# Second chunk's carried part of a state-space mixer from (C times B) times values instead of a chunk state, and a re-ordered drain

## The chip, the cores and the metric

One core of a Trainium2 chip runs the whole kernel: one launch, one program on five engines (TensorE = PE, VectorE = DVE, ScalarE = ACT, GpSimd = POOL, SyncE = SP) that meet at semaphores. The metric is device microseconds from start to end.

## The reference, cut to what matters

16 sequences of 256 tokens go through an embedding with attention, a state-space mixer (Mamba-2 style) and a mixture of eight experts. The change touches the mixer's scan `_ssd`: a sequence is two chunks of 128 tokens, with 8 heads of 64 channels and a state of 128.

```python
Y_diag = jnp.einsum('bcln,bcsn,bhcls,bcshp->bclhp', Cc, Bc, Lm, Xc)
decay_states = jnp.exp(a_cs[..., -1:] - a_cs)
states = jnp.einsum('bcln,bhcl,bclhp->bchpn', Bc, decay_states, Xc)
states = jnp.concatenate([jnp.zeros_like(states[:, :1]), states], axis=1)
...
prev_states = jnp.einsum('bhzc,bchpn->bzhpn', decay_chunk, states)[:, :-1]
Y_off = jnp.einsum('bcln,bchpn,bhcl->bclhp', Cc, prev_states, jnp.exp(a_cs))
return (Y_diag + Y_off).reshape(b, l, h, p)
```

With two chunks only the second has a carried part: exp(a_cs) * C2 (B1^T (decay * X1)), where 1 and 2 are the chunks. It is then gated, normalised, projected and added to the residual; then a router picks two of eight experts for each token, rows are scattered to slots in HBM, and each expert runs two products over its slots.

## The kernel before, in words

**Two parts.** The first handles one batch (a sequence of 256 tokens) after the other, in a software pipeline; the second (`experts`) runs the eight experts. Between them lies the drain: the last batch's mixer and routing, the scatter of its rows, and the load of the first expert's rows.

**The pipeline.** Each engine's program is a function `half(p, f, b, t, nf)`, called by `run_batches`. In one half, batch `f` is at its front (attention, input projection, convolution), batch `b`, the one before, is in its middle (the scan, the gate, the output projection), and `t`, two before, at its tail (routing, scatter). `q = 1 - p` is the buffer set of batch `b`. The order of work on an engine is the order in which `half` calls the helpers, and nothing but semaphores moves it. Halves with `f` and `b` are the steady loop, 15 of them; a half with `b` but no `f` is the first half of the drain, and one with neither its last.

**One half on PE, in order** (names are the helpers'): `query_side`, `project_z`, `scores`, `state_inputs` (L1593 transposes B of chunk 1, L1595 makes C B^T inside both chunks, L1597 the running sums), `x_to_rows`, `values`, `segment_sums` 0 and 1, `attend` (L1534, waits for `v` from DVE), `to_v2T`, `segment_sums` 2, `route`, `segment_sums` 3, `chunk_state` (L1633, B1^T times decayed values into bank 3), `own_chunk` 0 (L1643, the part inside chunk 1), `to_hT` (L1495 on `hn`), `from_state` (L1650, C2 times the state into bank 2), `own_chunk` 1, `choices_before`, `to_yT` 0 (L1495 on `y`, waits for the gated `y` of chunk 1 from DVE), `project_dt`, `project_channels`, `to_yT` 1, `project_out`.

**One half on DVE:** `query_max` (L1042, right behind `scores`), `mask_scores` (L1147), `scale_v` (L1051), `times_dt`, `decay_scores` (L1164: decays times the masked scores, one of 128x1024 for each chunk), `norm_1`, `router_in` and `router_top` (small), then `first_y` (L1177 and the gate L1171: y of chunk 1), `carried_y` (L1183: exp(a_cs) times what `from_state` made), `split_hT` (L1066), `second_y` (L1190, L1193 and the gate L1171), `slots_of`, `embedded`, `conv` in three groups among the small steps of a softplus, and `residual`.

**ACT** copies between banks and SBUF: `state_inputs` takes the transposed B to `bs` (L824; in the drain `state_copy`, L815), and `state` the state to `st` (L738). **POOL** makes the decayed values (`decayed_x`, L581), multiplies the values with D (`skip_x`, L588), makes segment inputs, takes roots (`gated_root`, L594), and describes and scatters rows (`describe_rows`, L612 to L616; `scatter_rows`, L625, four indirect DMAs for a batch).

`keep_clock` is a run of PE products whose result nobody reads. The last one before the experts stands behind the transposes of the first expert's rows (L1862).

## Time and profile before

| what | value |
|---|---|
| median of 3 runs | 926.17 us (925.28 to 926.82) |
| the profiled execution | 926.9 us, its span 925.2 us |
| busy, PE / PE weight loads | 904.3 us (98%) / 806.5 us (87%) |
| busy, DVE / ACT / POOL | 633.4 (68%) / 528.6 (57%) / 503.8 (54%) us |
| batches in a steady loop | from 41 to about 500 us |
| drain and start of the experts | from about 500 to 549 us |
| experts | from 549 us to the end; PE busy for 371.9 of the 372.0 us from 549 to 921 |

A busy share is a sum of the spans in which the engine shows an instruction. PE instructions overlap in the trace, so what one costs PE is read from the start of one group to the start of the next. An entry such as `[0.47 <-ACT hn L759]` at the end of a row says that the engine stood idle for 0.47 us before it, and what ended that. A matmul of four-byte floats shows as two records, so x16 in a PE row is eight products.

### The profile page before, as it was taken

How to read it: one execution, taken by the hardware profiler on the slowest of the kernel's cores; microseconds unless marked ns; L12 is line 12 of the kernel's file. 1: busy time of each engine (PE TensorE's matmuls, PEld its weight loads, DVE VectorE, ACT ScalarE, POOL GpSimd, SP SyncE). 2: the span in 40 equal slices, each digit the busy share in tenths (PEclk: the TensorE clock that was granted, in tenths of full speed). 3: DMA queues.
4: the chain of work that ended last, by engine and by line, in shares of the span. 5: the costliest groups of instructions: out<-in, count | busy, mean ns of one | idle time of the engine just before them, and what ended most of it. 6: DMA issues, size and time to landing. Idle time of an engine off the chain costs nothing. (4 is left out here: it accounts for less than half of the span.)

```text
span 925.2 us, 17776 instructions
## 1 busy us (share of the span) xinstructions
PE 904.3 (98%) x5832; PEld 806.5 (87%) x5832; DVE 633.4 (68%) x1698; ACT 528.6 (57%) x1097; POOL 503.8 (54%) x498
## 2 busy tenths in 40 slices
PE   8999999999999999999999979999999999999998
PEld 7888798888888888888888779999999999999997
DVE  1587889888988898889889644646464646464633
ACT  1767776677667766776667434444443434343533
POOL 5656877887778777876775522223232323232343
PEclk9999999999999999999999989999999999999999
DMA  7940011001000000000000044343434342523221
GB/s 211 321 154 17 30 47 34 23 34 34 13 23 14 24 13 23 14 25 12 12 14 5 25 138 122 70 109 74 108 70 112 67 115 63 119 58 79 23 58 46
DMA packets 49398, 59.13 MB, mean 64 GB/s; under 512 B 6304, under 2 KB 44683, under 8 KB 49360
## 3 DMA queue, kind: packets, MB, share of 16 engines
q1 hardware_dynamic: 35920, 42.14, 14.1%
q0 software_dynamic: 13440, 16.50, 10.7%
q8 instruction: 21, 0.34, 0.2%
q14 instruction: 17, 0.14, 0.1%
HBM read 33.62 MB, written 30.67 MB: 69 GB/s over the span
## 5 line engine op out<-in xcount | busy, mean ns | idle before, releaser
L690 POOL DMA_INDIRECT out<-ye,tok_slot x56 | 96.0, 1713 | 250.0 <-DMA out<-ye,tok_slot 128.0
L973 ACT ACTIVATE hf<-bank 128x512 f32<-128x512 f32 x128 | 79.3, 620 | 187.1 <-PE bank L1814 187.0
L1423 DVE TENSOR_TENSOR h_lo<-hf,h_hi 128x512 fp32r<-128x512 f32 x128 | 88.8, 694 | 101.5 <-ACT h_hi L975 100.1
L1812 PE MATMUL bank<-w_hi,h_hi 128*128 128x256 f32 x512 | 146.1, 285 | 0.0
L1813 PE MATMUL bank<-w_lo,h_hi 128*128 128x256 f32 x512 | 144.9, 283 | 0.0
L1814 PE MATMUL bank<-w_hi,h_lo 128*128 128x256 f32 x512 | 144.9, 283 | 0.0
L1122 DVE SCALAR_TENSOR_TENSOR xc<-bank,cw,xc 128x253 f32<-128x253 f32 (+2 forms) x288 | 128.2, 469 | 1.9 <-ACT xc L799 0.4
L1812 PE MATMUL bank<-xe_hi,w_hi 128*128 128x512 f32 x256 | 100.0, 391 | 0.0
L1813 PE MATMUL bank<-xe_lo,w_hi 128*128 128x512 f32 x256 | 99.8, 390 | 0.0
L1814 PE MATMUL bank<-xe_hi,w_lo 128*128 128x512 f32 x256 | 99.7, 389 | 0.0
L1813 PEld LDWEIGHTS bank<-w_lo,h_hi 128*128 128x128 f32 x512 | 98.3, 192 | 0.0
L1812 PEld LDWEIGHTS bank<-w_hi,h_hi 128*128 128x128 f32 x512 | 98.2, 192 | 0.0
L1814 PEld LDWEIGHTS bank<-w_hi,h_lo 128*128 128x128 f32 x512 | 98.2, 192 | 0.0
L625 POOL DMA_INDIRECT slots_dram<-rows,slot x64 | 63.7, 995 | 57.4 <-DVE slot L1271 35.7
L975 ACT ACTIVATE h_hi<-bank 128x512 fp32r<-128x512 f32 x128 | 79.4, 620 | 0.0
L1643 PEld LDWEIGHTS bank<-xdt,seg 128*128 128x128 f32 x512 | 61.0, 192 | 17.2 <-issue 16.5
L1440 DVE TENSOR_SCALAR ye<-bank,w_slot 128x256 f32<-128x256 f32 x58 | 27.9, 481 | 60.3 <-PE bank L1814 58.2
L573 POOL TENSOR_TENSOR seg_hi<-tri,a_hi 128x1024 fp32r<-128x1024 f32 x31 | 58.7, 1895 | 6.5 <-DVE a_lo L1107 6.5
L1643 PE MATMUL bank<-xdt,seg 128*128 128x64 f32 x512 | 60.9, 272 | 0.0
L799 ACT ACTIVATE xc<-bank,cb,cw 128x256 f32<-128x256 f32 x96 | 48.2, 563 | 20.6 <-PE bank L1550 18.7
L1662 PE MATMUL bank<-w_out,yT 128*128 128x256 f32 x256 | 58.2, 379 | 1.1 <-ACT yT L738 1.1
L573 POOL TENSOR_TENSOR seg_lo<-tri,a_lo 128x1024 fp32r<-128x1024 f32 x31 | 58.7, 1894 | 0.0
(223 smaller groups left out, 2352.3 us busy)
## 6 DMA issues: line engine op xcount, KB each, us to landing
w_raw<-w SPq DMA_DIRECT2D x16, 1024.0 KB
slots_dram<-zero_row SPq DMA_DIRECT2D x1, 8320.0 KB, 29.9
xe<-slots_dram SPq DMA_DIRECT2D x15, 520.0 KB, 4.5
out<-hb SPq DMA_DIRECT2D x16, 256.0 KB, 2.1
w_raw<-in_wT SPq DMA_DIRECT2D x2, 644.0 KB, 6.2
out<-zero_row SPq DMA_DIRECT2D x1, 1024.0 KB, 32.1
slots_dram<-rows,slot POOLq DMA_INDIRECT x64
out<-ye,tok_slot POOLq DMA_INDIRECT x64
```

What stands on the lines that cost most here:

```text
L573: ins = g.tensor_tensor(part[p][:, c, :, :], bc(tri[:, :].unsqueeze(1), [P, NH, P]), bc(a_part[p][:, c, :].unsqueeze(2).bitcast(F32), [P, ...
L625: g.indirect_dma_start(slots_dram, bass.IndirectOffsetOnAxis(ap=slot[p][:, 2 * c + k:2 * c + k + 1], axis=0), rows[p][:, c, :], None, boun ...
L690: g.indirect_dma_start(out, bass.IndirectOffsetOnAxis(ap=tok_slot[q][:, j:j + 1], axis=0), ye[q][:, j, :], None, compute_op=ALU.add).then_ ...
L973: sc.activation(hf[m % 2][:, :], h_bank[i % H_BANKS][:, :], ACT.Gelu_apprx_tanh)\
L975: sc.activation(h_hi[:, m, :], h_bank[i % H_BANKS][:, :], ACT.Gelu_apprx_tanh)\
L1122: ins = vc.scalar_tensor_tensor(out=xc[p][:, m, back:], in0=bank[p][XBC_BANK[i]][:, h * L:(h + 1) * L - back], scalar=cw[:, m, TAPS - 1 - ...
L1423: vc.tensor_tensor(h_lo[:, m, :], hf[m % 2][:, :], h_hi[:, m, :].bitcast(F32), ALU.subtract)\
L1643: ins = te.matmul(bank[p][YD_BANK[c]][:, h * HD:(h + 1) * HD], seg[p][:, c, h, :], xdt[p][:, c, h * HD:(h + 1) * HD], start=True, stop=True)
L1662: ins = te.matmul(bank[where][0][:, c * DM:(c + 1) * DM], yT[p][:, c, k, :], w_out[:, k, :], start=(k == 0), stop=(k == KI - 1))
L1812: te.matmul(out_, hi, rhi, start=first_, stop=False)
L1813: te.matmul(out_, hi, rlo, start=False, stop=False)
L1814: return te.matmul(out_, lo, rhi, start=False, stop=last_)
```

## The change

1. PE: `state_inputs` no longer transposes B of chunk 1. In its place it makes B1 times C2, a 128x128 product, in the same part of bank 3. ACT copies it as before, now to `across`.
2. PE: `chunk_state` becomes `across_chunks`. It multiplies `across` with the decayed values into bank 3, and that is at once the carried part. `from_state` is gone, and on ACT the copy `state` to `st`.
3. DVE: `carried_y` reads bank 3, and stands ahead of `first_y`, in the steady loop and in the drain.
4. The drain, POOL: `gated_root` of the last batch but one moves from the last steady half to behind `decayed_x`; `skip_x` waits until DVE has finished the decay products of both chunks; the last batch's rows are described by DVE, between `router_top` and `slots_of`, not by POOL.
5. The drain, PE: the last `keep_clock` before the experts has 3 products instead of 6.

```diff
@@ POOL, half: the drain @@
                     if b:
                         decayed_x(b, q)
+                        gated_root(t, p)
+                        pool.wait_ge(m_ready[KD - 1][q], m_ready[KD - 1].now(b, q))
                         skip_x(b, q, 0)
                         skip_x(b, q, 1)
                         pool.wait_ge(y_ready[q], y_ready.now(b, q))
...
                         second_root(b, q)
-                    describe_rows(t, p)
+                        describe_rows(t, p)
                     scatter_rows(t, p)
                     return
...
                 if not nf:
                     segment_inputs(f, p, 0)
-                    gated_root(b, q)
                     free_rows(t, p)
                     return
@@ ACT @@
             def state_inputs(r, p):
                 act.wait_ge(btg_psum[p], btg_psum.now(r, p))
-                sc.activation(bs[p][:, :], bank[p][3][:, 0:NS], ACT.Copy)
+                sc.activation(across[p][:, :], bank[p][3][:, 0:P], ACT.Copy)
...
-            def state(r, p):
-                act.wait_ge(state_psum[p], state_psum.now(r, p))
-                copy(st[p][:, :], bank[p][3][:, :], st_ready[p])
@@ DVE @@
                     dve.wait_ge(yo_psum[p], yo_psum.now(r, p))
-                    carried_y.last = back.mark(vc.tensor_tensor(heads(y[p][:, 1, :]), heads(bank[p][2][:, :]),
+                    carried_y.last = back.mark(vc.tensor_tensor(heads(y[p][:, 1, :]), heads(bank[p][3][:, :]),
...
+                def describe_rows(t, p):
+
+                    dve.wait_ge(tok_next[1 - p], tok_next.now(t, 1 - p))
+                    dve.wait_ge(ohs_ready[p], ohs_ready.now(t, p))
+                    vc.tensor_copy(rows[p][:, :, C_TOK].bitcast(I32), tok_iota[:, :])
+                    vc.tensor_copy(rows[p][:, :, C_E0], topf[p][:, :, 0])
+                    vc.tensor_tensor(rows[p][:, :, C_W0:C_W0 + 2], top[p][:, :, 0:2],
+                                     bc(linv[p][:, :].unsqueeze(2), [P, KD, 2]), ALU.mult).then_inc(row_info[p], 1)
...
                 if b:
+                    carried_y(b, q)
                     first_y(b, q)
-                    carried_y(b, q)
                 if f:
                     split_hT(f, p)
...
+                if not f:
+                    describe_rows(t, p)
                 if t:
                     slots_of(t, p)
@@ PE @@
                     pe.wait_ge(a_ready[p], a_ready.now(r, p))
-                    te.transpose(bank[where][3][:, 0:P], xc[p][:, KI, 0:P], ident[:, :])
+                    te.matmul(bank[where][3][:, 0:P], xc[p][:, KI, 0:P], xc[p][:, KI + 1, P:2 * P], start=True, stop=True)
...
-                def chunk_state(r, p):
+                def across_chunks(r, p):
...
-                    te.matmul(bank[p][3][:, :], bs[p][:, :], xdec[p][:, :], start=True, stop=True)\
-                        .then_inc(state_psum[p], 1)
+                    te.matmul(bank[p][3][:, :], across[p][:, :], xdec[p][:, :], start=True, stop=True)\
+                        .then_inc(yo_psum[p], 1)
...
-                def from_state(r, p):
-                    pe.wait_ge(st_ready[p], st_ready.now(r, p))
-                    pe.wait_ge(decay_ready[p], decay_ready.now(r, p))
-                    te.matmul(bank[p][2][:, :], xc[p][:, KI + 1, P:2 * P], st[p][:, :], start=True, stop=True)\
-                        .then_inc(yo_psum[p], 1)
...
-                    keep_clock(0, 6)
+                    keep_clock(0, 3)
```

The steady loop on PE, from the chunk state to the transposes of y (`hn` is the normalised front input, `seg` the decays times scores, a row with `waits` names the semaphores). Before:

```order
L1633 MATMUL bank<-xdec,bs 128x512 [waits xdec_ready,bs_ready,decay_ready]
L1643 MATMUL bank<-xdt,seg 128x64 [waits xdt_ready,xs_ready,m0_ready]
L1643 MATMUL bank<-xdt,seg 128x64 x7
L1495 MATMUL bank<-ident,hn 128x128 [waits hn_ready]
L1495 MATMUL bank<-ident,hn 128x128 x3
L1649 REGISTER_ALU [waits st_ready]
L1650 MATMUL bank<-st,xc 128x512 [waits decay_ready]
L1643 MATMUL bank<-xdt,seg 128x64 [waits m1_ready]
L1643 MATMUL bank<-xdt,seg 128x64 x7
```

And now:

```order
L1636 MATMUL bank<-xdec,across 128x512 [waits xdec_ready,bs_ready,decay_ready]
L1646 MATMUL bank<-xdt,seg 128x64 [waits xdt_ready,xs_ready,m0_ready]
L1646 MATMUL bank<-xdt,seg 128x64 x7
L1498 MATMUL bank<-ident,hn 128x128 [waits hn_ready]
L1498 MATMUL bank<-ident,hn 128x128 x3
L1646 MATMUL bank<-xdt,seg 128x64 [waits m1_ready]
L1646 MATMUL bank<-xdt,seg 128x64 x7
```

The product with the state is gone from between the transposes of `hn` and the second chunk's own part.

The same part of the steady loop on DVE, behind the router's small steps. Before:

```order
L1249 TENSOR_TENSOR ohs<-oh 128x16 [waits routing_chain]
L1177 TENSOR_TENSOR y<-bank,xs 128x512 [waits skip_ready,yd_psum]
L83 REGISTER_ALU [waits sz_ready]
L1171 TENSOR_TENSOR y<-y,sz 128x512 [waits back_chain]
L1183 TENSOR_TENSOR y<-bank,ea 128x512 [waits yo_psum]
L1066 TENSOR_TENSOR hT_lo<-hn,hT_hi 128x512 [waits hT_ready]
```

And now:

```order
L1241 TENSOR_TENSOR ohs<-oh 128x16 [waits routing_chain]
L1175 TENSOR_TENSOR y<-bank,ea 128x512 [waits yo_psum]
L1169 TENSOR_TENSOR y<-bank,xs 128x512 [waits skip_ready,yd_psum]
L1163 TENSOR_TENSOR y<-y,sz 128x512 [waits back_chain,sz_ready]
L1058 TENSOR_TENSOR hT_lo<-hn,hT_hi 128x512 [waits hT_ready]
```

The carried part stands one place earlier, and the first chunk's sum and gate one place later.

The drain on POOL, at the last batch's decayed values. Before:

```order
L594 TENSOR_TENSOR rms<-msq,neg_half 128x2 [waits msq_ready]
L581 TENSOR_TENSOR xdec<-xdt,edec 128x512 [waits scattered1,xdt_ready,edec_ready]
L588 TENSOR_TENSOR xs<-xs,dskip 128x512 [waits xs_ready] x2
L605 TENSOR_TENSOR hb<-h,bias_b 128x512 [waits h2_ready,hb_stored1,y_ready]
```

And now:

```order
L579 TENSOR_TENSOR xdec<-xdt,edec 128x512 [waits scattered1,xdt_ready,edec_ready]
L592 TENSOR_TENSOR rms<-msq,neg_half 128x2 [waits msq_ready]
L586 TENSOR_TENSOR xs<-xs,dskip 128x512 [waits xs_ready,m1_ready]
L586 TENSOR_TENSOR xs<-xs,dskip 128x512 [waits xs_ready]
L603 TENSOR_TENSOR hb<-h,bias_b 128x512 [waits h2_ready,hb_stored1,y_ready]
```

The root has moved behind the decayed values, and the products with D wait for `m1_ready`, which DVE gives behind its second decay product.

## Rows read from the trace of the kernel before

**Rows 1.** Windows: length, busy us (instructions) of PE, PEld, DVE, ACT, POOL; then PEclk, DMA
```profile
41.00:474.90 433.90, 429.75 (x2729) 374.23 (x2728) 373.22 (x1169) 309.87 (x669) 329.80 (x337) 1.00 0.11 33
532.00:549.00 17.00, 12.27 (x89) 11.69 (x88) 7.06 (x23) 4.87 (x9) 5.79 (x10) 0.80 0.44 142
```

**Rows 2.** Timeline of PE, one turn: start us, us, what [idle before]
```profile
323.17 1.99 PE L1534 MATMUL bank<-v,probs 128*128 128x256 f32 x8
...
330.99 0.66 PE L1495 MATMUL bank<-ident,hn 128*128 128x128 f32 x4 [0.47 <-ACT hn L759]
331.55 1.12 PE L1650 MATMUL bank<-st,xc 128*128 128x512 f32 x2
332.51 1.89 PE L1643 MATMUL bank<-xdt,seg 128*128 128x64 f32 x16
...
334.37 0.63 PE L1495 MATMUL bank<-ident,y 128*128 128x128 f32 x4
...
350.57 0.27 PE L1593 MATMUL bank<-ident,xc 128*128 128x128 f32 x1
350.68 0.61 PE L1595 MATMUL bank<-xc 128*128 128x128 f32 x4
...
351.74 1.89 PE L1516 MATMUL bank<-wv,xT 128*128 128x256 f32 x8
...
354.49 1.99 PE L1534 MATMUL bank<-v,probs 128*128 128x256 f32 x8
```

**Rows 3.** Timeline of DVE, the same turn
```profile
332.06 0.68 DVE L1177 TENSOR_TENSOR y<-bank,xs 128x512 f32<-128x512 f32 x1
332.78 0.69 DVE L1171 TENSOR_TENSOR y<-y,sz 128x512 f32<-128x512 f32 x1
333.39 0.68 DVE L1183 TENSOR_TENSOR y<-bank,ea 128x512 f32<-128x512 f32 x1
333.99 0.68 DVE L1066 TENSOR_TENSOR hT_lo<-hn,hT_hi 128x512 fp32r<-128x512 f32 x1
...
350.78 0.68 DVE L1042 TENSOR_REDUCE nmax<-bank 128x2 f32<-128x512 f32 x1
```

**Rows 4.** Timelines of DVE and PE, the turn behind it
```profile
363.32 0.68 DVE L1177 TENSOR_TENSOR y<-bank,xs 128x512 f32<-128x512 f32 x1
...
364.83 0.64 PE L1495 MATMUL bank<-ident,y 128*128 128x128 f32 x4
...
385.25 1.99 PE L1534 MATMUL bank<-v,probs 128*128 128x256 f32 x8
```

**Rows 5.** Timeline of DVE, end of the first full turn
```profile
71.34 0.69 DVE L1042 TENSOR_REDUCE nmax<-bank 128x2 f32<-128x512 f32 x1 [1.62 <-PE bank L1525]
```

**Rows 6.** L1164 over all turns (ns min/median/max); timelines in the drain, last batch's scan
```profile
L1164 DVE TENSOR_TENSOR seg<-seg,gm x32: 1224/1230/2115, 45.8 to 509.9; 128x1024 f32<-128x1024 f32 x32
...
507.96 4.04 DVE L1164 TENSOR_TENSOR seg<-seg,gm 128x1024 f32<-128x1024 f32 x2
508.90 4.01 POOL L588 TENSOR_TENSOR xs<-xs,dskip 128x512 f32<-128x512 f32 x2
...
513.50 0.69 DVE L1171 TENSOR_TENSOR y<-y,sz 128x512 f32<-128x512 f32 x1
```

**Rows 7.** Timelines of DVE and POOL in the drain, the last scatters
```profile
532.49 0.17 DVE L1271 TENSOR_SCALAR slot<-sl 128x4 int32<-128x4 f32 x1
532.57 0.98 POOL L625 DMA_INDIRECT slots_dram<-rows,slot  x1 [0.30 <-issue]
...
534.98 0.99 POOL L625 DMA_INDIRECT slots_dram<-rows,slot  x1 [0.82 <-issue]
```

**Rows 8.** Timelines of PE and DVE at the start of the experts
```profile
546.12 2.77 PE L1482 MATMUL bank<-ident 128*128 128x128 f32 x12
546.99 0.69 DVE L1451 TENSOR_TENSOR xe_lo<-bank,xe_hi 128x512 fp32r<-128x512 f32 x1
...
548.54 0.59 PE L1812 MATMUL bank<-xe_hi,w_hi 128*128 128x512 f32 x1
```

More of the change, by code:

```diff
@@ L237, in lm_block @@
         gm = pair("gm", [P, KD, P])
-        bs = pair("bs", [P, NS])
+        across = pair("across", [P, P])
         xdec = pair("xdec", [P, DI])
-        st = pair("st", [P, DI])
         h2 = pair("h2", [P, KD, DM])
@@ L327, in lm_block @@
         m_ready = [signal(f"m{c}_ready") for c in range(KD)]; skip_ready = signal("skip_ready", 2)
-        state_psum = signal("state_psum"); st_ready = signal("st_ready")
         yd_psum = signal("yd_psum", 2); yo_psum = signal("yo_psum")
@@ L814, in state_copy @@
                 act.wait_ge(btg_psum[p], btg_psum.now(r, p))
-                sc.activation(bs[p][:, :], bank[1 - p][3][:, 0:NS], ACT.Copy)
+                sc.activation(across[p][:, :], bank[1 - p][3][:, 0:P], ACT.Copy)
                 copy(ea[p][:, :], bank[1 - p][3][:, 3 * P:3 * P + NH], bs_ready[p])
@@ L890, in half @@
                     late_rows(b, q)
-                    state(b, q)
                     square(b, q, 0)
@@ L933, in half @@
                     normed(f, p)
-                if b:
-                    state(b, q)
                 if f:
@@ L1331, in half @@
                 if b:
+                    carried_y(b, q)
                     first_y(b, q)
-                    carried_y(b, q)
                 if f:
@@ L1713, in half @@
                     keep_clock(p, DRAIN["state"])
-                    chunk_state(b, q)
+                    across_chunks(b, q)
                     own_chunk(b, q, 0)
-                    from_state(b, q)
                     own_chunk(b, q, 1)
@@ L1767, in half @@
                     segment_sums(b, q, 3)
-                    chunk_state(b, q)
+                    across_chunks(b, q)
                     own_chunk(b, q, 0)
@@ L1773, in half @@
                     to_hT(f, p)
-                if b:
-                    from_state(b, q)
                 if b:
```

## The prediction

> **What bounds the kernel now.** I read the stretches first. The experts keep PE busy throughout, and the change touches no instruction of theirs; they only begin sooner or later. In the steady loop PE is busy for 429.75 of 433.90 us and DVE for 373.22 [rows 1]. That looks like PE alone, so that a product taken from PE would come off the time. I then read the timelines of PE and DVE beside each other over two turns, to see who is late for whom. The reader is to follow three points of a turn: `attend` (start 323.17, 354.49, 385.25), the start of the y steps on DVE (332.06 and 363.32, call it Y), and the first transposes of y on PE (334.37 and 364.83) [rows 2 to 4].
>
> - From `attend` to Y: 8.89 and 8.83 us.
> - From Y to the transposes of y: 2.31 and 1.51 us. DVE has the gated y of chunk 1 at 332.78 + 0.69 = 333.47, which is Y + 1.41 [rows 3]. So in the second turn PE begins as soon as DVE is done; in the first it comes 0.9 us later than it could.
> - From the transposes of y to `values`: 351.74 - 334.37 = 17.37 us of PE work with no idle entry, and from there to the next `attend` 2.75 us [rows 2].
> - DVE goes from Y to `query_max` in 350.78 - 332.06 = 18.72 us [rows 3], without an idle entry as well.
>
> So two chains go round, PE's and DVE's, within half a microsecond of each other, and `attend` waits for whichever is later. Two turns take 385.25 - 323.17 = 62.08 us, 31.04 each. From Y to `attend` it is 22.43 us in one and 21.93 in the other, mean 22.18. In the second the PE chain would have allowed 1.51 + 17.37 + 2.75 = 21.63; what it took, 21.93, is the DVE chain. I take 21.93 as the floor that DVE sets.
>
> **The product with the state (steady loop).** Removed from PE: from its start to the next group's, 332.51 - 331.55 = 0.96 us [rows 2]. Added: a product for a transpose in `state_inputs`. The transpose holds PE for 350.68 - 350.57 = 0.11 us; two products behind it last 0.61 us together with their tail, so one is at most 0.30 [rows 2]. The addition is 0.11 to 0.19; I take 0.11, since the tail overlaps the next group. Net 0.85 us off PE for each batch. The product itself lies between `to_hT` and the own part of chunk 2, ahead of the transposes of y.
>
> Without it PE reaches the transposes of y at 334.37 - 0.96 = 333.41, Y + 1.35, or sooner, because the idle 0.47 us before `to_hT` [rows 2] is not in every turn. But the change puts `carried_y` ahead of `first_y`. It holds DVE for 333.99 - 333.39 = 0.60 us [rows 3], and the y of chunk 1 is now done at Y + 0.60 + 1.41 = Y + 2.01. With 0.06 us for the semaphore PE begins at Y + 2.07. **PE stands still for 0.7 us or more, and in the second kind of turn it begins 0.56 us later than it does now.** The rest is 17.37 + 0.11 + 2.75, so `attend` comes at Y + 22.30. That is above DVE's floor of 21.93. A turn is 8.86 + 22.30 = 31.16 us against 31.04: 0.12 us longer. Bounds: DVE's floor, 8.86 + 21.93 = 30.79, 0.25 shorter; and everything as in the first kind of turn with the addition on top, 8.89 + 22.43 + 0.19 = 31.51, 0.47 longer. I take the middle value because each of its terms has its row. There are 13 such turns (`attend` of the third batch to that of the sixteenth): **+1.6 us** (-3.3 to +6.1).
>
> The first full turn is different. There `query_max` waited 1.62 us for PE [rows 5], so DVE has room and the 0.85 us comes off: **-0.8 us** (0 to -0.85).
>
> The copy of the state on ACT goes away and gives nothing: ACT waits for PE right behind it, for the transposes of `hn`. `across_chunks` is the old first product with other operands, so it costs the same. The carried part is there long before DVE asks for it: it is made ahead of `own_chunk` 0.
>
> **The drain: skips behind the decay products.** Now DVE's two decay products take 4.04 us for two, while POOL's two skips take 4.01 beside them [rows 6]. Over all turns the same DVE instruction takes 1.23 us in the median, and 2.1 at most [rows 6]: 0.8 us of its 2.0 here is a wait for POOL. With the skips held back, the second decay product ends about 0.8 us sooner. Not all of it arrives: `first_y` needs the first skip, about 1.0 us of POOL behind `m1_ready`. On DVE there lie the residual sum and now `carried_y` in that time, about 1.4 us, so they cover it. The gate of chunk 1, at 513.50 now [rows 6], would come at about 513.1 to 513.3; the second y gains about 1 us, but PE only asks for it behind the first projection. I take **-0.5 us** for the chain up to the last batch's rows, between 0 (the skips then just push `first_y`) and -1.05. The root that moves is 0.7 us of POOL between `decayed_x` and the wait for DVE, and nobody waits for it there.
>
> The decay product and the skips take turns rather than share, 1.0 us each. The Trainium skill says so of the shared port in "SBUF — State Buffer", section "SBUF: two separate sides": a DVE operation with two inputs in SBUF and a GpSimd operation exclude each other for a whole instruction. By that rule the moved skips would now meet the gate of chunk 1, also of two SBUF inputs, and hold it until the second skip ends; that would leave 0.3 us of the gain and make the time 0.2 us later. I stay with -0.5, inside its range.
>
> **The drain: rows described by DVE.** POOL's fourth scatter starts at 532.57 and lasts 0.98; the fifth starts at 534.98 [rows 7]. Otherwise the next starts 0.30 us behind the end of one, at 533.85. Four small POOL instructions and a wait go away: 534.98 - 533.85 = **-1.1 us**. The last batch's slots are ready at 532.66 [rows 7], and half a microsecond sooner with the step before, so they cover. On DVE the three small operations lie where it waits 1.0 us for PE's counts. Range -0.8 to -1.1, if the slots are late next.
>
> **The last keep_clock.** Six products now take 548.54 - 546.12 = 2.42 us at the low clock, 0.40 each; the split of the rows that the first expert product needs ends at 546.99 + 0.69 = 547.68 [rows 8]. With three, PE is done at 547.3 and waits until about 547.74: 0.8 us sooner. But the stretch has a mean granted clock of 0.80 [rows 1]: 17 us x 0.20 / 0.5 = 6.8 us at 1.2 GHz, and the rise to 2.4 GHz lies about where the products begin now. Up to 1 us of expert products would run at half speed and give 0.5 us back. I take **-0.4 us** (-0.8 to +0.8, if the clock rises later after the small pause). The Trainium skill, "TensorE: Matmul & The Clock Gate", section "Why this matters for your kernels", has continuous work on PE as the way to the full clock; by it the three products taken away are work that counts towards the rise. It speaks against this edit, and would make the time up to 0.8 us longer rather than 0.4 shorter.
>
> **Sum.** +1.6 - 0.8 - 0.5 - 1.1 - 0.4 = -1.2 us. The profiled execution of before would go from 926.9 to 925.7. Its time stands 0.7 us above the median of 926.17, so the median to compare with goes to **925.0 us**. A measurement of this kernel tells about 0.2%, 1.9 us, from no change, and this lies within it.
>
> **Rivals.**
>
> *DVE alone sets the turn (B).* The wait for y is absorbed because PE needs less than I read. Then the turn is 30.79 us: 13 x -0.25 = -3.3, with the rest -2.8: -6.1 us, 920.1. For it: half of the turns already run at that floor. Against it: 17.37 us is the same number in both kinds, so it is PE work and not waiting. Chance 0.2.
>
> *PE is the bound, and all of its saving arrives (C).* 0.85 x 14 = -11.9, with -2.0 of the drain: -13.9, 912.3. For it: 98% busy. Against it: DVE has no idle entry between Y and `query_max`. The Trainium skill, "Perfetto Trace Analysis", section "Identifying the Most-Contended Engine", has one look for the engine of the highest occupancy and work on it; by that rule this is the case. Chance 0.04.
>
> *Slower: POOL's skips fall in front of DVE's second decay product in every turn (D).* The place is the decay product of chunk 2 in the steady loop, behind `attend`. In the drain it took 2.0 us with POOL ahead [rows 6]; the price is 0.8 us where the router's small steps do not absorb it. It decides if `attend` to Y grows from 8.86 to over 9.2 us. At half the price, 0.4 x 13 = +5.2 on top of -1.2: +4.0, 930.2. For it: `attend` moves later against `query_max`, and POOL's roots hang on the latter. Against it: both kinds of turn had the same 8.8 to 8.9 us. Chance 0.12.
>
> *The edits of the drain do not add up (E):* only the scatters gain, the rest is hidden behind PE's projections: 13 x 0.12 - 0.8 - 1.1 = -0.3, 925.9. Chance 0.1, no change.
>
> **How the numbers follow.** The forecast has 0.54, with its own range 923 to 927; a third of it lies more than 1.9 us below the median of now. Faster: 0.18 + 0.2 (B) + 0.04 (C) = 0.42. Within 0.2%: 0.36 + 0.1 = 0.46. Slower: 0.12 (D). The range reaches down to B, 920.3, and up to 928.2, where the forecast's turn would be 0.25 us longer than I say; C and most of D stay out.
>
> **What the changed profile would show.** Right: PE idle about 0.7 to 1.4 us before the transposes of y in every turn, ended by DVE's gate; Y to `attend` near 22.3 us in all turns, no more alternation; turns of 31.1 to 31.2 us; in the drain decay products of 2.0 and 1.2 us; 0.3 us between the fourth and fifth scatter; the first expert product about 1.6 to 2.4 us closer to the drain's start. Wrong: turns below 31.0 us, with `attend` waiting for v behind `query_max` (B) or no idle before y's transposes (C); `attend` to Y above 9.2 us (D); a pause of the clock that reaches far into the experts.

## The result and the profile after

The changed kernel takes **938.43 us** in the median of four runs (935.2, 935.6, 941.27, 952.05) against 926.29 for the kernel before (925.28 to 926.82); the ratio is 1.012, with a 95% interval of 1.007 to 1.017. The run of 952.05, at the lowest granted clock of the four (0.969), is left out of the ratio, and the other three have a median of 935.6. So the change makes the kernel slower by 1.2%, where I forecast no change or a small gain, and the time lies above my range (920.3 to 928.2). The profiled execution took 935.6 us with a span of 933.9, against 926.9 and 925.2.

The head of the changed kernel's page:

```profile
span 933.9 us, 17711 instructions
...
PE 899.7 (96%) x5810; PEld 810.8 (87%) x5810; DVE 633.5 (68%) x1701; ACT 520.5 (56%) x1081; POOL 495.7 (53%) x494
```

PE's busy time went down from 904.3 to 899.7 us, and the span went up by 8.7. The windows of the changed kernel show in which stage: length, busy us (instructions) of PE, PEld, DVE, ACT and POOL, then the granted clock (PEclk), DMA share, GB/s.

```profile
74.39:487.34 412.95, 396.54 (x2536) 352.98 (x2536) 351.63 (x1106) 282.47 (x612) 304.44 (x322) 0.98 0.08 23
487.34:514.17 26.83, 25.49 (x165) 22.84 (x165) 22.35 (x72) 17.02 (x38) 14.65 (x17) 0.94 0.01 3
514.17:538.24 24.07, 21.89 (x158) 19.17 (x158) 18.19 (x53) 11.08 (x22) 10.36 (x15) 1.00 0.07 23
538.24:556.93 18.69, 14.49 (x111) 13.47 (x110) 8.38 (x34) 6.45 (x12) 7.89 (x8) 0.91 0.39 126
```

The first window is the 13 turns from the `attend` of the third batch to that of the sixteenth. It is 412.95 us long; before it was 403.56 (75.06 to 478.62). The granted clock there is 0.98, where before it was 1.00 [rows 1]. From the last `attend` to the end it is 446.5 us in both kernels. The whole loss lies in the loop, and the granted clock is lower there.

Nine of the 13 turns (from one `attend` to the next) take 31.11 to 31.44 us, mean 31.25. The other four take 32.88, 32.98, 32.98 and 32.89. First one of the nine, from its `attend` at 138.37 on: timeline of PE.

```profile
146.17 0.66 PE L1498 MATMUL bank<-ident,hn 128*128 128x128 f32 x4 [0.46 <-ACT hn L758]
...
149.39 0.66 PE L1498 MATMUL bank<-ident,y 128*128 128x128 f32 x4 [0.72 <-DVE y L1163]
149.88 0.96 PE L1562 MATMUL bank<-w_dt,hn 128*128 128x8 f32 x8
...
166.91 1.89 PE L1519 MATMUL bank<-wv,xT 128*128 128x256 f32 x8
...
169.66 1.99 PE L1537 MATMUL bank<-v,probs 128*128 128x256 f32 x8
```

And DVE in the same turn:

```profile
147.25 0.68 DVE L1175 TENSOR_TENSOR y<-bank,ea 128x512 f32<-128x512 f32 x1
147.85 0.68 DVE L1169 TENSOR_TENSOR y<-bank,xs 128x512 f32<-128x512 f32 x1
148.64 0.69 DVE L1163 TENSOR_TENSOR y<-y,sz 128x512 f32<-128x512 f32 x1
```

This is the turn that was foretold: the y steps start at `attend` + 8.88, the transposes of y come 2.14 later, then 17.52 and 2.75. The chunk-1 part of y stands behind `carried_y`, and PE waits 0.72 us for it (1.24 to 1.29 in the nine turns where `hn` came without a wait, all four slow ones among them); before, no transposes of y in the loop waited [rows 2, 4].

Now a slow turn, PE's timeline from 114.97 on:

```profile
114.97 0.17 PE L1693 MATMUL bank<-oh_sum,ones_b 128*128 128x8 bf16 x1
116.40 0.66 PE L1498 MATMUL bank<-ident,y 128*128 128x128 f32 x4 [1.27 <-DVE y L1163]
116.90 0.96 PE L1562 MATMUL bank<-w_dt,hn 128*128 128x8 f32 x8
...
118.26 0.28 PE L1553 MATMUL bank<-hT_hi,w_in_lo 128*128 128x256 f32 x1
118.38 0.34 PE L1553 MATMUL bank<-hT_lo,w_in_hi 128*128 128x256 f32 x1
118.52 0.41 PE L1553 MATMUL bank<-hT_hi,w_in_hi 128*128 128x256 f32 x1
118.73 0.42 PE L1553 MATMUL bank<-hT_hi,w_in_lo 128*128 128x256 f32 x1
```

The channel products stand 0.12 us apart up to 118.38 and 0.21 behind it. The windows say why:

```profile
115.00:118.40 3.40, 2.13 (x24) 2.04 (x21) 3.19 (x5) 1.56 (x4) 2.77 (x6) 1.00 0.37 61
118.50:121.80 3.30, 3.30 (x18) 3.30 (x17) 2.48 (x10) 1.44 (x5) 0.66 (x1) 0.50 0.08 17
122.00:125.00 3.00, 3.00 (x26) 2.95 (x25) 2.84 (x14) 1.51 (x3) 2.13 (x3) 1.00 0.25 89
```

From 118.5 to 121.9 the granted clock is at 1.2 GHz, and 2.4 GHz on both sides. The trace has five such stretches of 3.4 us, at 118.5, 214.0, 309.6, 435.9 and 500.8 us, each 2.0 to 2.3 us behind the start of y's transposes; before had none up to 541.96. Four are the slow turns, each about 1.7 us longer; the fifth lies behind the last `attend` and lengthens its window (26.83 us at a clock of 0.94; 25.42 us before).

At another place, between the last scatters and the experts, both kernels have a stretch at 1.2 GHz: 6.8 us from 541.96 before, 3.4 us from 548.6 in the changed kernel.

### The profile page after: what moved, and what is told of

It is laid out like the page before. It is cut to its first block, busy times and chain, and to the rows that moved or that the text cites. A ratio compares the mean times of both kernels' runs of the same rounds, so it can differ in the third digit from the quotient of the medians.

```text
span 933.9 us, 17711 instructions
## 1 busy us (share of the span) xinstructions
PE 899.7 (96%) x5810; PEld 810.8 (87%) x5810; DVE 633.5 (68%) x1701; ACT 520.5 (56%) x1081; POOL 495.7 (53%) x494
## 4 chain that ended last, share of the span: by engine, by line
PE 81%; DVE 9%; issue 4%; ACT 3%; POOL 1%; PEld 1%; another core or an unknown queue 0%; DVEq 0%; POOLq 0%; ACTq 0%
PE bank L1806 13%; PE bank L1807 13%; PE bank L1808 13%; PE bank L1553 12%; PE bank L1659 6%; PE bank L1498 5%; PE bank L1537 3%; PE bank L1528 3%; PE bank L1519 3%; PE bank L1617 3%; PE bank L1512 3%; PE bank L1562 1%; PE bank L1818 1%; PE bank L1680 1%; DVE y L1163 1%
## 5 line engine op out<-in xcount | busy, mean ns | idle before, releaser
L798 ACT ACTIVATE xc<-bank,cb,cw 128x256 f32<-128x256 f32 x96 | 48.7, 561 | 30.4 <-PE bank L1553 21.8
L1553 PE MATMUL bank<-hT_hi,w_in_hi 128*128 128x256 f32 x192 | 61.1, 318 | 0.0
```

What stands on the lines that cost most here:

```text
L1553: ins = te.matmul(dst, *((w_, h_) if transposed else (h_, w_)), start=first_ and n == 0, stop=last_ and n == 2)
```

## Experiments

Theory from here on: the pause before y's transposes lets the clock fall, and nothing else in the change costs. "Drops" are stretches at 1.2 GHz in the loop of the profiled execution, one that falls behind the transposes of y after the last `attend` included. Y is the start of the y steps on DVE. A row of waits has PE's line, the instruction waited for, then us in total, times, and the longest in us.

**E1: the old order of the y steps (in the drain too), the rest as changed.** The product with the state wrote bank 2, the new carried part is in bank 3, where chunk 1's y is transposed; that is what ties `carried_y` to the front. So the transposes go to bank 2, and `to_xT` also waits for `carried_y`.

```diff
-        XS_BANK, YD_BANK, YT_BANK = (2, 1), (1, 0), (3, 1)
+        XS_BANK, YD_BANK, YT_BANK = (2, 1), (1, 0), (2, 1)
...
-                    carried_y(b, q)
                     first_y(b, q)
+                    carried_y(b, q)
...
                         pe.wait_ge(yT_ready[q], yT_ready.now(b, q, 1))
+                        pe.wait_ge(back_chain, Chain(pe, back_chain, BACK_LINKS, b, q).value(2))
```

> The changed kernel with the old order of the y steps (first_y, then carried_y; the transposes of chunk 1's y go to bank 2, since bank 3 still holds the carried part, and to_xT waits for carried_y). Theory 1, the clock: PE's pause of 1.3 us before the transposes of y is what pulls the granted clock down in some turns. Here the pause shrinks to about 0.7 us (the gated y comes at Y + 1.4, PE is there at Y + 0.6), so the drops go away, a turn is DVE's 30.8 us, and the median is 920 to 923 us. Rival, theory 2: any pause of PE near this size drops the clock, or the saving of PE is what makes PE look idle: then low stretches stay in the loop, and the time is above 926 us although the turns without a drop take 30.8 us.

Measured: **920.53 us** (919.72 to 921.09), ratio 0.9945 [0.9929, 0.9962]. No drop. Turns of 30.69 to 31.01 us, the transposes of y 1.47 us behind the y steps' start. Waits of PE from 75 to 478 us, the window, and a turn:

```profile
PE bank L1498 <- ACT hn L758: 5.6, 12, 0.5
PE bank L1498 <- DVE y L1163: 0.8, 2, 0.6
```
```profile
75.00:478.00 403.00, 395.86 (x2548) 348.07 (x2547) 352.96 (x1106) 282.58 (x613) 317.94 (x323) 1.00 0.08 23
```
```profile
205.44 0.66 PE L1498 MATMUL bank<-ident,hn 128*128 128x128 f32 x4 [0.47 <-ACT hn L758]
...
207.99 0.66 PE L1498 MATMUL bank<-ident,y 128*128 128x128 f32 x4
```

The pause has moved ahead of the transposes of `hn`, it is there in 12 of the 13 turns, and the clock stays at 2.4 GHz. This version beats both kernels. Its span is 7.2 us shorter than that of the kernel before: 2.3 in the loop, 0.9 ahead of it and 4.0 behind it, where it has no stretch at 1.2 GHz ahead of the experts.

**E2: the changed kernel with five idle products in the pause.**

```diff
                 if b:
+                    for _ in range(5):
+                        te.matmul(bank[q][2][:, 0:P], ident[:, :], ident[:, :], start=True, stop=True)
                     to_yT(b, q, 0)
```

> The changed kernel with five products that nobody reads (128x128, into bank 2 of the batch) ahead of the transposes of chunk 1's y, in the steady loop: they fill about 1.1 of the 1.3 us in which PE waits for DVE. Nothing that others wait for moves. Theory 1, the clock: no low stretch in the loop, all turns 31.2 us, median 926 us or up to 1.5 below. Rival, theory 2: the time is lost by the later y itself or by other waits, the clock only follows: then the turns stay mixed, 31.2 and 32.9 us, and the median stays at 935 to 941 us.

Measured: **927.04 us** (926.28 to 928.7), ratio 1.0015 [1.0006, 1.0025]. No drop. PE's timeline:

```profile
115.44 1.36 PE L1776 MATMUL bank<-ident 128*128 128x128 f32 x10
116.85 0.66 PE L1498 MATMUL bank<-ident,y 128*128 128x128 f32 x4
```

Turns are 31.11 to 31.23 us, as in the changed kernel's turns without a drop, and the transposes still come at Y + 2.13. Five products that compute nothing and shorten nothing take 9.3 us off the span (933.9 to 924.6): 7.6 in the loop and 2.1 behind it, with 0.4 more ahead of it. The dependencies and the place of y are those of the changed kernel, so this isolates the clock. (One of its ten executions, 928.7 us, ran at a mean clock of 0.994, the others at 0.996 to 1.000.) (A product of four-byte floats is two records; one is 0.22 us here, and five fill 1.1 us. The 0.11 us that I gave for one in E5, E7 and E9 is wrong.)

**E3: the kernel before with only `carried_y` put ahead of `first_y`.**

> The kernel before with carried_y ahead of first_y and nothing else. PE still has the product with the state, so its pause before the transposes of y should be 0.5 us or less in one kind of turn and 0.6 in the other. Theory 1: the clock stays at 2.4 GHz in the loop; a turn grows from 31.04 to 31.2 to 31.5 us (y is 0.6 us later, and in half of the turns PE was waiting for it), median 928 to 932 us. Rival: the order alone makes low stretches as the whole change does: above 934 us.

Measured: **935.55 us** (932.52 to 938.1), ratio 1.0094 [1.0074, 1.0115]. Five drops. I was wrong, the rival right. Waits and a window of PE, and the pause ahead of the first drop (at 149.9):

```profile
PE bank L1495 <- DVE y L1171: 5.0, 13, 0.5
PE bank L1495 <- ACT hn L759: 1.9, 4, 0.5
```
```profile
75.00:478.00 403.00, 396.11 (x2496) 346.50 (x2495) 343.11 (x1081) 279.96 (x608) 296.29 (x314) 0.98 0.08 23
```
```profile
148.19 0.66 PE L1495 MATMUL bank<-ident,y 128*128 128x128 f32 x4 [0.50 <-DVE y L1171]
```

Turns without a drop take 31.0 us, with one 32.8 to 32.9, and the turn behind one 31.8. So two lines in another order, with all products kept, cost about as much as the whole change (9.3 us; its spans are 936.4 against 933.9). And E3 has as much of PE's waiting in the loop (403.00 - 396.11 = 6.9 us) as E1 (7.1 us), which had no drop. The total of the pauses does not decide: the four slow turns of E3 each have one pause, 0.37 to 0.50 us ahead of y, and the turns of E1 have about 0.5 us in all.

**E4: the kernel before with only the edits of the drain** (skips behind the decay products, rows described by DVE; six idle products as before).

> The kernel before with the edits of the drain on POOL and DVE alone: the moved root, the skips behind the decay products, the last rows described by DVE. The last keep_clock keeps its six products. From the changed kernel's trace: 0.5 us at the first scatter and 1.2 us among the scatters, 1.7 us in all, so a median of 924.6 us; the clock in the loop is as before. Rival: the experts' start does not follow the scatters (PE comes late out of its 38 filling products), then 926 us.

Measured: **924.99 us** (924.37 to 925.52), ratio 0.9987 [0.9977, 0.9996]. The scatters come 1.28 to 1.37 us apart throughout. In this execution the stretch at 1.2 GHz ahead of the experts is missing as well, so part of the gain may be the clock's. E1 differs from E4 by the product, its banks and the shorter `keep_clock`, so the product in the right order is worth 4.5 us.

**E5: E3 with three idle products** ahead of the transposes of y (edit as in E2, in another bank), and **E6: the changed kernel with two instead of five.**

> The kernel before, with carried_y ahead of first_y as in the order-alone run, and three idle 128x128 products (0.11 us each, 0.33 in all) into a free bank ahead of the transposes of y in each turn. The order-alone run took 935.55 us, with five stretches at 1.2 GHz behind a pause of 0.4 to 0.5 us at this place. Theory 1 (the clock made nearly all of that loss): no stretch at 1.2 GHz in the loop, turns of 31.0 us as in the turns of the order-alone run without one; 31.0 against 31.04 now for 13 turns is nothing, so 926 to 928 us. Theory 2 (the order costs by DVE alone, and the clock is a bystander): 934 us or more, since the fillers take nothing off DVE. If three products are too few, some of the five stretches stay, 1.7 us each.

> The changed kernel with two idle 128x128 products ahead of the transposes of y where the run with five had none of the stretches at 1.2 GHz: the pauses there go from about 0.66 and 1.27 us to about 0.4 and 1.0 us. Theory 1 (what counts is how long PE is without work at this place): the pauses left are as long as those of the order-alone run (0.4 to 0.5 us), which had five stretches, so 3 to 5 stay and the time is 932 to 938 us. Rival (a few products at this place are enough whatever pause is left): no stretch, 927 us as with five.

Measured, E5: **932.01 us** (929.59 to 932.05), ratio 1.0061 [1.0044, 1.0078]. No drop in the profiled execution (929.59 us). Turns are 31.18 us: three products are 0.66 us, 0.2 more than the pause. That is 13 x 0.14 = 1.8 us over before, and the first full turn is 0.7 longer (30.62 against 29.90): 2.5, which is also the difference of the spans (927.7 against 925.2). The three other executions took 932.0 us, at a mean granted clock of 0.994 against 0.996; what lay between them and the profiled one no trace shows. Theory 1 holds for the drops of the profiled execution, but the median is 4 us above what I gave.

E6: **932.71 us** (930.45 to 936.8), ratio 1.0061 [1.004, 1.0081]. Four drops and one in the drain, at 524.8; the waits of PE for y that are left:

```profile
PE bank L1498 <- DVE y L1163: 7.2, 13, 0.7
```

Its four executions took 936.8, 933.2, 932.22 and 930.45 us at mean granted clocks of 0.987, 0.993, 0.992 and 0.994. The mean clock, and with it, as I read it, the number of drops, differs from execution to execution. That fits the scatter: 5.6 and 6.4 us in E3 and E6, 6.1 in the changed kernel, 1.2 to 3.2 in the others. The changed kernel itself: 935.6 and 935.2 us at 0.989 and 0.987, 941.27 at 0.979.

**E7: E1 with six idle products ahead of the first expert product** in place of three.

> The version with the old order of the y steps (920.53 us), with six idle products again ahead of the first expert product instead of three. With three, PE waited 1.1 us there for DVE's split, at the full clock. Theory 1 (this edit is worth nothing, since three products of 0.11 us fit into the wait): 920.5 us, the wait shorter by 0.33 us, the clock unchanged. Rival (the prediction's step): 0.4 us later, 920.9, or more if the clock is low there and each product takes 0.2 to 0.4 us.

Measured: 921.94 us (920.98 to 923.32), ratio 0.9956 [0.9941, 0.9971]; E1 had 0.9945 with an interval that overlaps. It doesn't separate them. PE in the two kernels, E1 first:

```profile
539.53 0.83 PE L1485 MATMUL bank<-ident 128*128 128x128 f32 x6
541.44 0.49 PE L1807 MATMUL bank<-xe_hi,w_hi 128*128 128x512 f32 x1 [1.08 <-DVE xe_lo L1454]
```
```profile
539.99 1.50 PE L1485 MATMUL bank<-ident 128*128 128x128 f32 x12
542.71 0.49 PE L1807 MATMUL bank<-xe_hi,w_hi 128*128 128x512 f32 x1 [1.21 <-DVE xe_lo L1454]
```

In both PE waits for DVE's split behind its idle products, so they aren't on the path there. From the eighth scatter to the first expert product it takes 8.56 (E1), 8.88 (E4, six) and 8.98 us (E2, three) where the clock is at 2.4 GHz there, and 9.64 to 10.54 (changed kernel, E6, E7, before) where a stretch at 1.2 GHz falls into it; where the stretch reaches past the first expert product it is 8.42 (E10) and 9.18 (E3). E7's falls at 533.9, before the edited products run.

**E8: the changed kernel with the dt products ahead of the transposes of y**, and **E9: the five idle products of E2 behind those transposes.**

```diff
-                if b:
-                    to_yT(b, q, 0)
                 if not b:
                     keep_clock(q, FILL["dt"])
                 if f:
                     project_dt(f, p)
+                if b:
+                    to_yT(b, q, 0)
+                if f:
                     project_channels(f, p, 0)
```

> The changed kernel, with PE's eight small dt products (0.81 us, now behind the transposes of y) put ahead of them, so that PE works through most of its pause. Nothing is added. The chain of PE behind the transposes becomes 0.81 us shorter: Y + 2.13 + 17.52 - 0.81 + 2.75 = Y + 21.59, below the 22.0 us that DVE needs (turns of 30.9 us in the run with the old order of the y steps). The pause goes from 0.7 to 1.3 us to 0 to 0.5. Theory 1 (the pause at this place pulls the clock down, and shortening it below what the old order left is enough): no or one stretch at 1.2 GHz, turns of 30.9 us, 920 to 922 us. Rival (it is the run of small products around this place that does it, whatever stands between them): three to five stretches, 2 us each on top, 926 to 931 us.

> The changed kernel with the same five idle 128x128 products as in the run that had no drop, but behind the transposes of y instead of ahead of them. The pauses of 0.7 to 1.3 us stay whole; only work is added, 5 x 0.11 = 0.55 us per turn on PE's chain, 7 us over 13 turns (turns of 31.75 us). Theory 1 (the length of the pause ahead of y decides): three to five stretches at 1.2 GHz as in the changed kernel, 942 to 946 us. Rival (the work of PE around this place decides, and the pause is only a part of it): no or one stretch, 933 to 936 us.

(The dt products are four, in eight records; they take 0.81 us together as stated.)

E8: **931.18 us** (929.55 to 932.7), ratio 1.005 [1.0033, 1.0067]. Three drops in the loop and one in the drain, at 520.2. The transposes of y no longer wait, and yet the clock falls; the rival was right on the drops, and the time is 0.2 us above its range. PE's waits:

```profile
PE bank L1498 <- ACT hn L758: 3.5, 7, 0.6
PE bank L1562 <- ACT hn L782: 3.4, 13, 0.3
```

What is left is a pause of 0.2 to 0.3 us, now between the router's and the dt products, both of 8 columns.

E9: **953.64 us** (952.59 to 955.7), ratio 1.0305 [1.0287, 1.0323]. No drop:

```profile
149.32 0.66 PE L1498 MATMUL bank<-ident,hn 128*128 128x128 f32 x4 [0.48 <-ACT hn L758]
...
152.54 0.66 PE L1498 MATMUL bank<-ident,y 128*128 128x128 f32 x4 [0.72 <-DVE y L1163]
153.03 1.28 PE L1777 MATMUL bank<-ident 128*128 128x128 f32 x10
```
```profile
75.54:474.00 398.46, 379.68 (x2468) 334.61 (x2468) 327.58 (x1022) 258.73 (x567) 285.22 (x301) 1.00 0.08 23
```

PE waits 0.72 us ahead of y in 12 of the 13 turns (1.24 in the first), longer than in E3, and more in all than in any other kernel (18.8 us of 398.5), at a full clock. So the theory that the length of the pause decides is refuted. The rival that work of 1.1 us beside the pause is enough fits, but is not shown alone: the turns also became 1.8 us longer. And the three other executions ran at mean granted clocks of 0.993 to 0.998, so some of them may have had drops. The time itself is far off both expectations: the turn is 33.1 us, not 31.75, because 1.11 us were added, not 0.55, and `attend` now follows `values` after 3.4 to 3.5 us instead of 2.75: it stands behind segment sums that wait for DVE (`gm`, 4.4 us in 12 waits), which came late with the turn.

**E10: E1 with the dt products ahead of the transposes of y** (edit as in E8).

> The version with the old order of the y steps (920.53 us, no stretch at 1.2 GHz in the loop, although PE pauses 0.5 us ahead of the transposes of hn in every turn), with one thing changed: PE's eight dt products (8 columns each) go ahead of the transposes of y. hT is 0.3 us late for them, as in the run with the dt products first. So a pause of about 0.3 us comes to lie among the smallest products, and nothing is added; DVE sets the turn as before. Theory 1 (a pause pulls the clock down where it lies among the products of 8 columns and the transposes of y, however short, and not at the transposes of hn): three to five stretches at 1.2 GHz, 926 to 931 us. Rival (the pause ahead of the transposes of y was what counted, or the total of the pauses: here about 0.8 us a turn, less than in the changed kernel): no stretch, 920.5 us.

Measured: **923.57 us** (921.96 to 924.83), ratio 0.9973 [0.9962, 0.9984]. One drop in the loop (at 271.8; that turn takes 32.37 us, the others 30.7 to 31.0). PE:

```profile
144.12 0.66 PE L1498 MATMUL bank<-ident,hn 128*128 128x128 f32 x4 [0.47 <-ACT hn L758]
...
146.45 0.17 PE L1693 MATMUL bank<-oh_sum,ones_b 128*128 128x8 bf16 x1
146.89 1.03 PE L1562 MATMUL bank<-w_dt,hn 128*128 128x8 f32 x8 [0.27 <-ACT hn L782]
147.78 0.63 PE L1498 MATMUL bank<-ident,y 128*128 128x128 f32 x4
```

A pause of 0.27 us at this place came with one drop, while 0.47 us ahead of `hn`, in the same turns, had brought none in E1. The median is 3 us above E1's; in the spans (920.6 against 918.0) the loop has 1.2 of the difference, and 1.1 lie behind it, in part because a stretch at 1.2 GHz from 541.5 on reaches into the experts. The time lies between both expectations: the place matters, but a pause this short brings fewer drops than I said.

All kernels side by side. "Pause" is PE's waiting in one turn between the router's products and the first channel product, "work beside it" what was added there; "+ 1" is a further drop in the drain (E6 at 524.8, E8 at 520.2), behind a wait of 0.78 us for the copy of the transposed y.

| kernel | pause, us | work beside it, us | drops | us |
|---|---|---|---|---|
| before / E4 | 0 | 0 | 0 / 0 | 926.3 / 925.0 |
| E1 | 0 (two turns up to 0.6) | 0 | 0 | 920.5 |
| E2 | under 0.1 | 1.1 | 0 | 927.0 |
| E5 | 0 | 0.66 | 0 | 932.0 (profiled 929.6) |
| E10 | 0.27 | 0 | 1 | 923.6 |
| E8 | 0.2 to 0.3 | 0 | 3 + 1 | 931.2 |
| E3 | 0.3 to 0.5 | 0 | 5 | 935.6 |
| E6 | 0.2 to 0.7 | 0.45 | 4 + 1 | 932.7 |
| changed kernel | 0.7 to 1.3 | 0 | 5 | 938.4 (935.6 without the run of 952.05) |
| E9 | 0.7 to 1.2 | 1.1 | 0 | 953.6 |

The table leaves out the stretch at 1.2 GHz around the last scatters and the load of the first expert's rows, 3.4 or 6.8 us long. E1, E2 and E4 have none; all the others have one. It makes the way from the last scatter to the first expert product, or the start of the experts, 0.6 to 2 us longer, so differences of 1 to 2 us between rows can come from it.

## Why the prediction was wrong

**The step that failed** is "PE stands still for 0.7 us or more", in the part on the product with the state. I had the pause, its cause and its length right (0.72 and 1.27 us), and priced it at its own length, 0.56 us in every second turn. Its other price, what the granted clock does behind it, was not in the sum; I thought of the clock only at the last `keep_clock`. It is 6.7 us in the loop, four turns of 1.68, and 1.4 us behind it. E2 confirms it: with the pause filled the same kernel takes 927.0 us. The "what would make it wrong" named a clock pause in the experts, not one in the loop. What I had weighed on the clock stood beside the wrong edit: the Trainium skill, "TensorE: Matmul & The Clock Gate", section "Why this matters for your kernels", has continuous work on PE as the way to the full clock. In the loop, work put into the pause kept the full clock (E2), but unbroken work is not needed for it: E1 had it with 7.1 us of waits in 403, E9 with 18.8 in 398. For the last `keep_clock`, where I named it, no run here shows an effect.

**The turn.** Predicted 31.16 us, from 8.86 + 2.07 + 17.37 + 0.11 + 2.75. The turns without a drop have 8.8 to 8.9, then 2.13 + 17.52 + 2.75; the mean is 31.25. Each term is within 0.07 us. Over 13 turns that is +2.7 instead of +1.6. The rest of the loop's loss is 4 drops of 1.68 us, 6.7; together 9.4, which is 412.95 - 403.56.

**The first full turn:** -0.8 foretold, -0.64 measured (29.26 us against 29.90).

**The skips behind the decay products:** -0.5 foretold, and -0.5 measured, by luck. From DVE's last `gm` to the first scatter it is 24.07 us (514.17 to 538.24), against 24.58 before. The two decay products take 3.25 us against 4.04 [rows 6], with the skips behind:

```profile
518.05 3.25 DVE L1156 TENSOR_TENSOR seg<-seg,gm 128x1024 f32<-128x1024 f32 x2
...
523.39 0.69 DVE L1163 TENSOR_TENSOR y<-y,sz 128x512 f32<-128x512 f32 x1
```
```profile
521.38 2.04 POOL L586 TENSOR_TENSOR xs<-xs,dskip 128x512 f32<-128x512 f32 x2 [0.62 <-DVE seg L1156]
```

But in E4, which has this edit with the old product and the old order, the stretch is 24.58 us: the second decay product takes 1.21 us there too, but nothing is gained, and `first_y` waits 0.44 us for the skip. In the changed kernel `carried_y` covers that wait, as I said, but the gain is not from there: E1 has the old order, the same wait of 0.44 us, and still only 24.00 us.

```profile
499.82 0.42 DVE L1139 TENSOR_TENSOR gm<-bank,tri 128x256 f32<-128x256 f32 x1 [0.93 <-ACT ea L737]
...
523.82 1.07 POOL L623 DMA_INDIRECT slots_dram<-rows,slot  x1 [2.21 <-DVE slot L1263]
```

What E1 has and E4 has not is the new product with its banks, so the 0.5 us belong to it, and the moved skips gave nothing. The new order alone costs here: 25.24 us in E3. The Trainium skill's rule on the shared port ("SBUF — State Buffer", section "SBUF: two separate sides") would, as I forecast it, have had the gate wait for the second skip. The gate starts at 523.39, 0.78 us behind the step ahead of it as in the kernel before, and the second skip ends at 523.42; so no wait shows here. The root that moved takes 1.71 us of POOL, not 0.7, but nobody waits for it, as foretold.

**The rows described by DVE:** -1.1 foretold, -1.2 measured (first to eighth scatter 9.05 us against 10.22), and E4 shows the same (9.07). The fifth scatter now follows after 0.30 us [rows 7]:

```profile
543.46 0.97 POOL L623 DMA_INDIRECT slots_dram<-rows,slot  x1 [0.30 <-issue]
```

**The last keep_clock:** -0.4 foretold; nothing measured. In the kernel before, where the six products ran at 1.2 GHz, PE came to the first expert product without a wait [rows 8]. But with three products and a stretch of 6.8 us as well, E6 and E8 take 10.54 and 10.43 us from the last scatter to that product, against 9.69 before. In the changed kernel PE came late out of its 38 idle products (it started them late itself, `issue`), and then stood for DVE:

```profile
549.70 4.02 PE L1485 MATMUL bank<-ident 128*128 128x128 f32 x25 [0.43 <-issue]
...
554.43 0.83 PE L1485 MATMUL bank<-ident 128*128 128x128 f32 x6
556.93 0.49 PE L1806 MATMUL bank<-xe_hi,w_hi 128*128 128x512 f32 x1 [1.67 <-DVE xe_lo L1454]
```

**The gains of the drain** were there, 1.7 us (0.5 of them from the product), and were given back by the fifth drop (1.4 us) and 0.3 us in the experts: 446.5 us from the last `attend` to the end in both kernels.

**The rivals.** B, DVE alone as the bound with turns of 30.79 us and 920.1 us, is not what the change does, but it is close to what E1 does: 30.86 us in the mean, 21.8 to 22.0 from Y to `attend` where I had read 21.93 as DVE's floor. My reading of the floor was right. That E1's 920.5 us lies so near B's 920.1 is in part luck: the loop gave 2.3 us, not 3.3, and the drain more than I had put there. If DVE is the floor, further savings on PE will not show in E1; no run tested that. D had the right sign and the wrong mechanism: `attend` to Y stayed at 8.7 to 9.1 us. C fell: 0.85 us off PE brought 0.18 us a turn at best. E was right on its part, the drain (the skips and the last `keep_clock` gave nothing, the scatters 1.2 us), and wrong in its time, since it had the same sum for the loop.

**What stays open.** The drops in the loop stand two to four turns apart, always at the same place (E10 has only one); why in these turns was not tested. The mean clock differs between executions, and the run of 952.05 us may be the same effect with more drops; it has no trace. Nor was it shown what of the work beside a pause counts, its columns or its time, nor what the longer turn did in E9. The Trainium skill, "TensorE: Matmul & The Clock Gate", section "What's actually happening", says that the chip watches PE's activity independently of where the program is, and that the same kernel differs from run to run for it. The first three drops of the changed kernel agree with it: they stand 95.57 us apart both times, while the turns that they fall into start 95.38 and 95.45 us apart.

## What to carry to other kernels

A pause of PE is not priced by its length alone. Where it falls among very small products (8 and 64 columns, transposes), 0.3 to 1.3 us cost about 1.7 us each time the clock falls behind it, while 0.5 us ahead of a block of other work brought no drop; so before a change opens a wait on PE, look at what PE does on both sides of it. When products are saved on an engine within half a microsecond of another, first ask which order keeps the freed time out of such a place: here the bank that the new result lives in forced the order, and another bank turned a loss of 9 to 12 us into a gain of 5.6. And the window view's clock column belongs beside every turn time: a loop at 0.98 instead of 1.00 was most of the result.

## What was not expected of the hardware

The granted clock fell for 3.4 us at a time behind pauses of only 0.2 to 1.3 us, in a loop that keeps PE busy for 96 to 98% of it, 0.6 to 2.3 us behind the start of y's transposes. Two kernels with the same sum of waits on PE (E1 7.1 us, E3 6.9 us in 403) had no drop and five. Five idle products of 0.22 us each, put ahead of the transposes (E2) or behind them (E9), kept the clock at 2.4 GHz in the loop of the profiled execution, in E9 even with 18.8 us of waits in 398; two of them did not (E6). The Trainium skill, "TensorE: Matmul & The Clock Gate", "Why this matters for your kernels", sees danger in longer gaps than these; where it and the traces differ, the traces decide.
